# Outer products grouped by tile width in the second layer of a four-layer graph network

## What is computed

```python
h = relu(layernorm(x))                      # [3125, 160]
xs, xv = split(h[src], 64, 32)              # per edge: 64 scalars, 32 x 3
es, ev = split(edge_attr_32, 8, 8)          # per edge: 8 scalars, 8 x 3
s1 = einsum('ea,eb,abc->ec',   xs, es, W1)  # out: 64 scalars
s2 = einsum('eai,ebi,abc->ec', xv, ev, W2)
v1 = einsum('ea,ebi,abc->eci', xs, ev, W3)  # out: 32 x 3
v2 = einsum('eai,eb,abc->eci', xv, es, W4)
messages = concat(s1 + s2, v1 + v2) @ Wm + bm   # scale factors left out
agg = segment_sum(messages, dst, 3125)
x = x + h + concat(h, agg) @ Wu + bu
```

## Time and profile before

| | us |
|---|---|
| median of 3 runs (lowest, highest) | 14113.39 (14100.84, 14146.35) |
| the profiled execution | 14119.49 |
| its span, first to last instruction | 14117.7 |
| PE busy in the span | 10464.4 (74%) |
| DVE, POOL, ACT busy | 8261.9, 7999.7, 4621.4 |
| mean granted TensorE clock | 0.853 |
| outer products of the second layer, first to last | 4548.5 to 7245.3 |

### The profile page before, as it was taken

How to read it: one execution, slowest core, us unless ns; L and a number is a source line. 1 busy time by engine, 2 the same in 40 slices (tenths; PEclk the granted TensorE clock), 3 DMA queues, 4 the chain that set the end, 5 groups by cost and what they waited for, 6 DMA issues and landing times. The chain is left out here.

```text
span 14117.7 us, 252258 instructions
## 1 busy us (share of the span) xinstructions
PE 10464.4 (74%) x61566; PEld 6640.3 (47%) x61567; DVE 8261.9 (59%) x26728; ACT 4621.4 (33%) x15914; POOL 7999.7 (57%) x12600
## 2 busy tenths in 40 slices
PE   4544444378885999999984666665888888888888
PEld 1000000056664444444443444422677777777776
DVE  6544444266664222222323444496888888888887
ACT  0000000045552111111111222100666676676675
POOL 3666666455553444444414656353677777777775
PEclk9999999988886565555656878786999999999998
DMA  4000000022222222222212222462100000000000
GB/s 122 23 23 23 23 23 22 10 59 58 58 58 43 48 49 48 47 48 48 49 24 68 73 71 73 83 117 46 25 22 21 21 21 21 21 21 21 21 21 21
DMA packets 901097, 598.03 MB, mean 42 GB/s; under 512 B 654029, under 2 KB 831011, under 8 KB 898312
## 3 DMA queue, kind: packets, MB, share of 16 engines
q0 software_dynamic: 235616, 359.73, 10.0%
q1 hardware_dynamic: 650440, 197.82, 7.8%
q10 hardware_dynamic: 14624, 35.51, 0.6%
HBM read 512.98 MB, written 79.56 MB: 42 GB/s over the span
## 5 line engine op out<-in xcount | busy, mean ns | idle before, releaser
L1237 POOL DMA_INDIRECT l1s_node_rows<-node_table,l1s_edge_rows x1216 | 1238.1, 1018 | 1501.1 <-DMA l1s_edge_rows<-rows_by_src 736.8
L1324 PE MATMUL l1s_p_outer<-l1s_edge_by_node,l1s_node_rows 128*32 128x64 f32 (+2 forms) x14592 | 1749.3, 345 | 204.2 <-issue 104.3
L1324 PEld LDWEIGHTS l1s_p_outer<-l1s_edge_by_node,l1s_node_rows 128*32 128x32 f32 (+2 forms) x14592 | 1026.7, 168 | 1058.7 <-issue 913.8
L503 PE MATMUL rank<-onehot,lower_h 128*128 128x427 f16 x812 | 437.5, 539 | 1400.3 <-remote 1069.1
L1572 POOL DMA_INDIRECT l2s_node_rows<-node_table,l2s_edge_rows x864 | 855.1, 990 | 877.0 <-DMA l2s_edge_rows<-rows_by_src 325.0
L516 POOL DMA_INDIRECT rows_by_src<-row_s,pos_i x812 | 821.6, 1012 | 786.0 <-issue 439.7
L796 POOL DMA_INDIRECT l_source_rows<-node_table,l_edge_rows x880 | 866.2, 984 | 683.7 <-DMA l_edge_rows<-rows_by_dst 398.1
L1348 ACT COPY l1s_outer<-l1s_p_outer 128x264 f32<-128x264 f32 x1216 | 449.2, 379 | 2326.8 <-PE l1s_p_outer L1324 1882.5
L481 DVE TENSOR_TENSOR before<-before,onehot 128x427 f16<-128x427 f16 x812 | 312.4, 385 | 1241.9 <-remote 1063.7
L2276 POOL DMA_INDIRECT l_source_rows<-node_table,l_edge_rows x866 | 847.7, 979 | 301.9 <-issue 236.5
L1268 DVE TENSOR_TENSOR l_sums_s<-l_sums_s,l1s_p_sums_s 64x8 f32 x1280 | 195.1, 152 | 1349.1 <-PE l1s_p_sums_s L1306 1057.1
(11 more groups left out here) (541 smaller groups left out, 28608.9 us busy)
## 6 DMA issues: line engine op xcount, KB each, us to landing
l_xv_by<-h_turned_l SPq DMA_DIRECT2D x120, 320.0 KB
l_source_rows<-node_table,l_edge_rows POOLq DMA_INDIRECT x1746
l_xs_by<-h_turned_l SPq DMA_DIRECT2D x40, 640.0 KB
l1s_edge_rows<-rows_by_src SPq DMA_DIRECT2D x1216, 19.5 KB
l1s_node_rows<-node_table,l1s_edge_rows POOLq DMA_INDIRECT x1216
rows_by_src<-pad_rows_s ACTq DMA_DIRECT2D x16, 1053.0 KB
l2s_edge_rows<-rows_by_src SPq DMA_DIRECT2D x216, 78.0 KB
l_edge_rows<-rows_by_dst SPq DMA_DIRECT2D x220, 72.0 KB
```

The source lines that it names most:

```text
L503: nc.tensor.matmul(rank[:, b, 0:BINS], K["lower_h"][:, :], onehot[:, b, :], start=True, stop=False)
L1237: pool.indirect_dma_start(xg[q][:, s, :], None, table, bass.IndirectOffsetOnAxis(ap=pay[q][:, s, S_DST:S_DST + 1].bitcast(U32), axis=0)).t ...
L1324: ins = nc.tensor.matmul(p_o[rows, j % RING, col:col + n], xg[q][:, s, lhs], rhs(eh[q % RING][:, s, :, :]), start=True, stop=True, skip_gr ...
```

## The change

- The outer products of four slots are issued as two groups: first the 64-wide ones of all four slots, then the 32-wide ones of all four. The wait for a free bank stands ahead of each slot's wide products; the count `outer` is raised after each slot's narrow ones.
- The 97-wide product is gone. Its vector parts go into the three 32-wide products, which now stream 128 columns (own part of the edge vector, and the edge scalars). The count of edges comes from a fourth 32-wide product with a stationary operand of ones, 8 columns streamed, at partition 96.
- The contraction is a list of steps: the four times three 32-wide products first (with the count product beside the first three), then the twelve products to the scalar sums in six pairs, one at partitions 0 to 63 and one at 64 to 127, then the eight 96-wide ones. The scalar sums thus come in two halves of partitions (`acc_s` has 128 partitions instead of 64), which `stage_update` adds up by weights that stand twice.

```diff
-    ZROWS = max(rows for _, rows, *_ in outers)
+    ZROWS = P
...
                 def contract(k, part):
 
                     ins = None
-                    for n, (to, rows, lhs, krows, b) in list(enumerate(products))[part]:
-                        zb = z[k][krows, b, :, :].rearrange("p s n -> p (s n)")
-                        ins = nc.tensor.matmul((c_s, c_v)[to][k][rows, 0:BATCH_S * G], lhs, zb, start=n == first[to], stop=n == last[to], skip_group_check=True)
+                    for tiles in products[part]:
+                        for to, rows, lhs, krows, b, first, last in tiles:
+                            zb = z[k][krows, b, :, :].rearrange("p s n -> p (s n)")
+                            ins = nc.tensor.matmul((c_s, c_v)[to][k][rows, 0:BATCH_S * G], lhs, zb, start=first, stop=last, skip_group_check=True)
                     return ins
...
                             for s in range(QUAD):
-                                j = q * QUAD + s
-                                pe.wait_ge(evacuated, it * BATCH_S + (j + 1))
-                                for rows, _, col, n, lhs, rhs in outers:
-                                    ins = nc.tensor.matmul(p_o[rows, j % RING, col:col + n], xg[q][:, s, lhs], rhs(eh[q % RING][:, s, :, :]), start=True, stop=True, skip_group_check=True)
+                                pe.wait_ge(evacuated, it * BATCH_S + (q * QUAD + s + 1))
+                                for rows, col, n, lhs, rhs in outers[0]:
+                                    nc.tensor.matmul(p_o[rows, s, col:col + n], lhs(xg[q][:, s, :]), rhs(eh[q % RING][:, s, :, :]), start=True, stop=True, skip_group_check=True)
+                            for s in range(QUAD):
+                                for rows, col, n, lhs, rhs in outers[1]:
+                                    ins = nc.tensor.matmul(p_o[rows, s, col:col + n], lhs(xg[q][:, s, :]), rhs(eh[q % RING][:, s, :, :]), start=True, stop=True, skip_group_check=True)
                                 ins.then_inc(outer, 1)
...
-    RS, RV, RH = CS, 3 * CV + 1, D - P
+    RS, RV, RH = 2 * CS, 3 * CV + 1, D - P
...
-                nc.tensor.transpose(turn[0][:, 0:RS], wm_s[:, 0:P], ident[0:RS, 0:RS])
+                for h in range(2):
+                    nc.tensor.transpose(turn[0][:, h * CS:(h + 1) * CS], wm_s[:, 0:P], ident[0:CS, 0:CS])
...
-        acc_s, acc_v = sb("sums_s", [CS, NP]), sb("sums_v", [3 * CV + 1, NP])
+        acc_s, acc_v = sb("sums_s", [P, NP]), sb("sums_v", [3 * CV + 1, NP])
...
-            A_, ES, ONE, EV = 0, 2 * NS, 3 * NS, 3 * NS + 1
-            flat = lambda e: e.rearrange("p c n -> p (c n)")
+            A_, EV, ES, ONE = 0, 2 * NS, 3 * NS, 4 * NS
+            scalars = lambda x: x[:, 0:CS]
             half = lambda t: lambda e: free(e[:, t * HALF, 0:1], [NS * G, 4], [1, HALF * G])
-            outers = [(slice(t * CS, (t + 1) * CS), P, A_ * G, 2 * NS * G, slice(0, CS), half(t)) for t in range(2)]
-            for i in range(3):
-                outers.append((V[i], P, EV * G, NS * G, slice(CS + CV * i, CS + CV * (i + 1)), lambda e, i=i: flat(e[:, NS * i:NS * (i + 1), :])))
-            outers.append((slice(0, 3 * CV + 1), P, ES * G, (NS + 1) * G, slice(CS, D + 1), lambda e: flat(e[:, 3 * NS:4 * NS + 1, :])))
+            axis = lambda i: lambda x: x[:, CS + CV * i:CS + CV * (i + 1)]
+            own_and_scalar = lambda i: lambda e: free(e[:, NS * i, 0:1], [(3 - i) * NS * G, 2], [1, NS * G])
+            wide = [(slice(t * CS, (t + 1) * CS), A_ * G, 2 * NS * G, scalars, half(t)) for t in range(2)]
+            narrow = [(V[i], EV * G, 2 * NS * G, axis(i), own_and_scalar(i)) for i in range(3)]
+            narrow.append((LAST, ONE * G, G, lambda x: ones[:, :], lambda e: e[:, 4 * NS, :]))
+            outers = [wide, narrow]
             ALL_V = slice(0, 3 * CV)
-            products = [(1, slice(0, 3 * CV + 1), one[:, :], slice(0, 3 * CV + 1), ONE)]
+            products = []
             for j in range(HALF):
-                products += [(1, V[i], xs_v[:, j, :], slice(0, P), A_ + HALF * i + j) for i in range(3)]
-                products.append((0, S0, xs_s[:, j, :], slice(0, P), A_ + HALF * 3 + j))
+                products.append([(1, V[i], xs_v[:, j, :], slice(0, P), A_ + HALF * i + j, j == 0, False) for i in range(3)])
+            products[0].append((1, LAST, one[:, :], slice(0, P), ONE, True, True))
+            to_scalar = [(xs_s[:, j, :], slice(0, P), A_ + HALF * 3 + j) for j in range(HALF)]
+            to_scalar += [(xv_s[:, b, :], ALL_V, EV + b) for b in range(NS)]
+            PAIRS = len(to_scalar) // 2
+            for n in range(PAIRS):
+                products.append([(0, slice(h * CS, (h + 1) * CS), *to_scalar[2 * n + h], n == 0, n == PAIRS - 1) for h in range(2)])
             for b in range(NS):
-                products.append((1, ALL_V, xv_v[:, b, :], ALL_V, ES + b))
-                products.append((0, S0, xv_s[:, b, :], ALL_V, EV + b))
+                products.append([(1, ALL_V, xv_v[:, b, :], ALL_V, ES + b, False, b == NS - 1)])
```

13 lines of the change are left out of this document (6 added, 7 removed).

## The result

The changed kernel took 13799.03 us (median of 4 runs, 13788.68 to 13825.86) where the kernel before took 14129.87 us (4 runs, the three behind the 14113.39 above and one more): a ratio of 0.976, 95% interval 0.9738 to 0.9783. Forecast were 13140 us and a range of 13050 to 13430. The direction was right; of 976 us expected, a third came.

A forecast was written before the change was run, and what follows sets the result against it. TensorE was taken as the bound at 70.2 us an iteration, POOL's gathers (42.9) next; 44.5 us an iteration over 38 saves 977 us, less 1, from 14119.5: 13143, rounded as run median to 13140 us, range 13050 to 13430.

The forecast's parts named there:

- Steps 1 to 3: TensorE in layer-two stage: four slots 3.75 us instead of 6.08; contraction 16.6 instead of 26.5; iteration 46.6 lower level, 24 upper.
- Rivals C and E: Outer products, contraction: C, array still drains, 13625 us, chance 0.05; E, four column groups not side by side, 14525 us, 0.02.
- Step 4: POOL's gather issue is late next: 32 x 1.34 = 42.9 us an iteration, whatever TensorE does.
- The sum: Stage iteration: larger of POOL's 42.9 us and TensorE's 24 to 46.6, taken as 44.5 instead of 70.2, over 38 iterations.
- rival B's term: TensorE stays the bound at lower clock, "issue" gaps surface: 46.6 to 52 us an iteration, 13220 to 13425 us; chance 0.20.
- Step 5: Wide products' waits for ACT's copies: late copy 0.78 us after the one before; covered at lower level, up to 1.5 us a quad at upper.
- Rival D: TensorE's instructions can't be supplied faster: 58 us an iteration, 13650 us; chance 0.05.
- The clock: TensorE's clock in the stage, 0.58 to 0.62: passes fill 91% rather than 58%, so more of the upper level expected.

The follow-up runs named there:

- e9: Changed kernel with gathers issued only in the first iteration and the grouping of four slots undone: 12992.68 us, ratio 0.8985 to the kernel before at 14458.44 us.
- e10: Changed kernel with gathers issued only in the first iteration and the contraction in single steps: 12958.98 us, ratio 0.8961 to the kernel before at 14458.44 us.
- e11: Changed kernel with its gathers replaced by plain SyncE transfers of as many bytes, same rows each time: 13278.27 us, ratio 0.9182 to the kernel before at 14458.44 us.
- e2: Kernel before with gathers issued only in the first iteration: 12229.85 us, ratio 0.9989 to the unaltered kernel before at 12242.12 us.
- e14: Changed kernel with ScalarE copying two banks by one instruction: 13817.30 us, ratio 0.9758 to the kernel before at 14158.03 us.
- e16: Changed kernel with one TensorE wait and one ScalarE copy per four slots instead of four each: 13801.74 us, ratio 0.975 to the kernel before at 14117.15 us.
- e1: Changed kernel with gathers issued only in the first iteration: 11513.12 us, ratio 0.9435 to the kernel before at 12242.12 us.
- e15: Changed kernel, gathers kept, with the contraction in single steps instead of pairs: 13900.57 us, ratio 0.9813 to the kernel before at 14158.03 us.
- e8: Changed kernel with a small fill and a wait for it after each gather on GpSimd: 13091.22 us, ratio 1.0698 to the kernel before at 12232.94 us.
- e7: Changed kernel unaltered, timed again: 12127.33 us, ratio 0.9905 to the kernel before at 12232.94 us.
- e6: Kernel before with ScalarE copying two banks by one instruction: 12240.26 us, ratio 1.001 to the unaltered kernel before at 12242.12 us.

## Why the prediction was wrong

**Steps 1 to 3, right.** Four slots take 3.50 us at the lower level (3.75 forecast), 1.99 at the upper (1.95); pairs are worth 4.6 us at the upper level; an iteration without gathers takes 27.4 us (24), 25.4 of them busy. Rivals C and E are out by the earlier trace rows against the rows from 5621.40: narrow products of four column groups side by side, 1.59 us for the group.

**Step 4, right as a floor, and reached in the short condition only.** 32 x 1.34 = 42.9 us was POOL's own time; measured 43.8. The forecast was made for the long condition, so this doesn't save it.

**What failed is the price put beside it.** The sum took an iteration as "the larger of 42.9 (POOL) and a TensorE time between 24 and 46.6 us", with 1.6 us on top for all that isn't overlapped. Measured are 62.0 us, above both, with TensorE idle for 19.8. In the long condition gathers and TensorE's work don't overlap freely: with gathers there are stretches in which the other engines are slow, without them there are none (e9, e10, e11), and the stretches are TensorE's loss. The step that held this was rival B's term: "104 us are 2.7 us an iteration; twice that on top gives the upper end". It measured 14.3 us of "issue" and 4.7 of late copies. My reading is that the 104 us were what was left over when a queue of slow passes had hidden the rest; to double it priced the remainder and not what was hidden. A sign of it stood in the trace of before, in views that the prediction didn't draw on: ACT waited 316.7 us for "remote", 85 times in that stage, and SyncE's queue 469.8. That this was hidden by slack and came out when TensorE's work was cut is argued, not shown: no run takes the gathers from the kernel before in the long condition. An estimate says how much can be new. If that kernel would take 45.1 us there without gathers, as in the short condition (e2), they cost it 70.9 - 45.1 = 25.8 us an iteration, almost all by the lower clock (0.60 against 0.99) and little by standing still (2.3 us). The changed kernel loses 62.0 - 27.4 = 34.6. The extra 8.8 us are half of the 45.1 - 27.4 = 17.7 that the change is worth without gathers.

**Step 5, wrong in size.** It priced a late copy at 0.78 us; in a stretch copies come 1.5 to 3.1 us apart. That the wide products wait for them is shown (178.6 us); that this is what costs the time isn't: with half, or a quarter, of the copies the time stays (e14, e16).

**Rival D** came nearest in time (13650 us against 13799) and named the right signature, "issue" as PE's releaser, but its reason falls: a limit of TensorE's supply would stay without gathers.

**The clock.** "I expect more of the upper level" was right, 0.60 to 0.72, and 0.98 without gathers. That full passes bring it isn't shown: the kernel before, with its thin passes, has 0.99 without gathers too (e2, short condition). The rows show this: without transferred node rows 0.98 to 0.99 in either condition (e1, e2, e9, e10); with gathers 0.70 to 0.95 in the short condition, where the paced gathers, and no slow stretch, go with the 0.70; with gathers 0.58 to 0.77 in the long one; with SyncE's transfers 0.86 (e11). What sets the level between these no run separates. The Trainium skill, page "TensorE: Matmul & The Clock Gate", section "Wait — 56ns, not 53.3ns?", gives some 62 ns of sequencer time per matmul where instructions are decoded in software. By that, 32 narrow records would have taken 1.98 us; they took 1.01 at the upper level (5608.48 to 5609.49), and e1 has 208 records in 10 us (4010 to 4020), 48 ns each. The measurement differs: either this isn't that case, or the figure doesn't hold here.

**Open.** Why the same program meets a long and a short condition no run shows. On record each set has a chip of its own: short on 2 and 7, long on 1, 6 and 4. So the condition may belong to the chip or to what else went on at the time; no chip was used in both. In the long condition the program is slower in other stages too: of the 1681 us between the changed kernel's two profiles (13786.9 and 12106.2), 693 lie ahead of this stage, 691 in it and 297 behind. Nor is it shown by what path a gather slows the other sequencers.

## What to carry to other kernels

When a bound is cut, ask not only which engine is next but what the old bound was hiding: add up the waits on all engines that end in "remote" or "issue", not those of the bound alone, since a small remainder on the bound says nothing of what its queue covers. And take gathers issued by GpSimd as work that can cost every engine time, here up to 1 us each, not GpSimd alone; whether the maximum or the sum of two engines' times holds can be told by one run with the gathers issued once, if it is timed in the condition that the forecast is for. Compare only kernels timed side by side: the same change was worth 2.4% in one condition and 0.9% in the other.

## What the runs showed of the hardware

- While gathers were issued in the long condition there were stretches in which PE started one product per 0.72 to 0.75 us with nothing to wait for, ACT's copies came 1.5 to 3.1 us apart and DVE stood for 7.5 us; 1.0 us was lost per gather (e15 against e10). With as many bytes moved by SyncE's transfers, of rows that lay together, there were none (PE waits of 2.8 us for "issue" in 1400). The Trainium skill, page "DMA: Bandwidth & Descriptors", section "SWDGE vs HWDGE vs iDMA", says that descriptors of GpSimd's transfers are written by its own cores into SBUF while SyncE's are made by hardware. By that rule the two kinds differ in GpSimd's part, which is the part that e11 takes away, and its trace has no slow stretch; that this writing is what holds up other engines no run here shows.
- A fill of 0.218 us with a wait for it between gathers cost 0.80 us on GpSimd (e8 against e7: 2.17 against 1.37 us a gather).
- The granted clock was 0.60 with TensorE busy 97% (before, long condition), 0.95 with it busy 99% (e6, short condition, with gathers) and 0.99 with it busy 99% (e2, short condition, without): here the busy share alone does not tell the level. With paced gathers (e8, short condition, PE waiting for node rows for 1020 of 2500 us) it was 0.70.
